# Edge counts of a graph attention from 16 buckets instead of 8 tiles, with one matmul per block of edges

## The reference, cut to what matters

```python
# x: (1024, 512); src, dst: (17408,) node numbers
edge_index = jnp.stack([src, dst])
xn = _layernorm(x, axis=-1)
q = xn @ Wq + bq;  k = xn @ Wk + bk;  v = xn @ Wv + bv
adj = zeros((N, N)).at[edge_index[0], edge_index[1]].set(1.0)
a = q @ k.T / sqrt(512)
a = a * adj + (1.0 - adj) * NEG
x = x + softmax(a, axis=-1) @ v
...
# a later stage, the same edges: neigh = segment_sum(feat[src], dst)
```

## Time and profile before

| | |
|---|---|
| runs | 1079.86, 1082.82, 1085.95 us; median 1082.82 |
| profiled execution | 1079.54 us, span 1077.7 us |
| granted TensorE clock, mean | 0.919 of full speed |
| TensorE busy | 887.4 us (82%) |
| VectorE busy | 758.5 us (70%) |
| ScalarE busy | 506.9 us (47%) |
| GpSimd busy | 357.5 us (33%) |
| first stage up to the first transpose of its attention | 246.8 us |

### The profile page before, as it was taken

One profiled execution on the slowest core, in us unless ns is written; L12 is line 12 of the kernel. 1 busy time (PEld: TensorE's weight loads), 2 busy tenths in 40 slices (PEclk: granted clock), 3 DMA queues, 4 the chain that ended last, 5 costly groups with the idle time before them and its releaser, 6 DMA issues.

```text
span 1077.7 us, 13803 instructions
## 1 busy us (share of the span) xinstructions
PE 887.4 (82%) x4522; PEld 676.1 (63%) x4522; DVE 758.5 (70%) x1555; ACT 506.9 (47%) x881; POOL 357.5 (33%) x236
## 2 busy tenths in 40 slices
PE   2999998888883999698898689899999987655990
PEld 2777773336762887377686567777767765434860
DVE  8879599886697443866223767788786867796638
ACT  3467517655653555122202146656565655543530
POOL 1000000000112553008320337786685666703520
PEclk9999999998986999599998899999999998967985
DMA  5110000007252443623210330020010140373442
GB/s 161 30 22 2 1 1 1 1 16 259 79 201 82 136 149 117 245 66 110 62 46 1 107 78 1 20 59 20 2 30 20 21 156 1 101 261 96 149 145 89
DMA packets 55524, 84.74 MB, mean 79 GB/s; under 512 B 8977, under 2 KB 31761, under 8 KB 54945
## 3 DMA queue, kind: packets, MB, share of 16 engines
q1 hardware_dynamic: 49376, 63.94, 19.0%
q0 software_dynamic: 6080, 19.93, 5.7%
HBM read 57.11 MB, written 22.54 MB: 74 GB/s over the span
## 4 chain that ended last, share of the span: by engine, by line
PE 56%; DVE 33%; ACT 4%; issue 4%; POOL 1%; DMA 1%; DVEq 0%; ACTq 0%; POOLq 0%
PE PS L328 36%; DVE late_columns L1153 4%; PE PS L1980 3%; PE PS L1995 3%; DVE neg_max L1553 3%; PE PS L1969 3%; DVE APL L987 2%; PE PS L1994 2%; DVE count_rows L1133 2%; PE PS L1888 2%; PE PS L1669 2%; PE PS L1831 2%; DVE early_columns L1153 1%; DVE XN L1024 1%; DVE stats L995 1%
## 5 line engine op out<-in xcount | busy, mean ns | idle before, releaser
L616 POOL TENSOR_SCALAR AP__201<-AP__201,rden 128x1024 f32<-128x1024 f32 x64 | 182.0, 2848 | 86.4 <-DVE rden L1558 85.8
L557 POOL TENSOR_TENSOR W1L<-W1R,W1H 128x1024 fp32r<-128x1024 f32 x8 | 18.9, 2404 | 291.5 <-DVE neg_max L1172 288.5
L648 ACT ACTIVATE APH<-PS 128x512 fp32r<-128x512 f32 x128 | 71.7, 597 | 70.2 <-PE PS L1980 45.7
L1553 DVE TENSOR_REDUCE neg_max<-PS 128x1 f32<-128x1024 f32 x64 | 78.3, 1223 | 36.9 <-PE PS L1969 36.0
L987 DVE TENSOR_TENSOR APL<-PS,APH 128x512 fp32r<-128x512 f32 x128 | 83.0, 680 | 23.8 <-ACT APH L648 23.6
L328 PE MATMUL PS<-XTH,WH 128*128 128x512 f32 x224 | 79.9, 403 | 4.5 <-DVE XTL L987 4.5
L1980 PE MATMUL PS<-ident,AP__201 128*128 128x128 f32 x512 | 71.2, 281 | 11.5 <-DVE APL L987 10.7
L1980 PEld LDWEIGHTS PS<-ident,AP__201 128*128 128x128 f32 x512 | 59.9, 144 | 28.2 <-issue 17.1
L328 PE MATMUL PS<-XTL,WH 128*128 128x512 f32 x224 | 77.2, 391 | 0.0
L328 PE MATMUL PS<-XTH,WL 128*128 128x512 f32 x224 | 77.0, 390 | 0.0
L928 ACT ACTIVATE AP__201<-PS,neg_max 128x1024 f32<-128x1024 f32 x64 | 71.5, 1117 | 7.3 <-DVE neg_max L1553 6.6
(11 more groups left out here) (302 smaller groups left out, 2422.1 us busy)
## 6 DMA issues: line engine op xcount, KB each, us to landing
YT<-expert_rows SPq DMA_DIRECT2D x12, 512.0 KB, 7.5
counts<-CT SPq DMA_DIRECT2D x8, 512.0 KB, 4.9
W1R<-in_L_ffn_w SPq DMA_DIRECT2D x8, 512.0 KB, 3.9
W2R<-in_L_ffn_w SPq DMA_DIRECT2D x8, 512.0 KB, 5.3
normalised<-XN SPq DMA_DIRECT2D x2, 2048.0 KB, 8.4
CG<-counts SPq DMA_DIRECT2D x8, 512.0 KB, 3.4
RAW<-in_L_gnn_W SPq DMA_DIRECT2D x16, 256.0 KB, 2.9
W1R<-in_L_ffn_W SPq DMA_DIRECT2D x8, 512.0 KB, 8.7
```

Of the source, the lines that this page charges most:

```text
L616: gp.tensor_scalar(AP_[:, i % 4, :], AP_[:, i % 4, :], rden[:, i % 4:i % 4 + 1], None, ALU.mult).then_inc(B["norm"], 1)
L648: act.activation(dst, src, Copy, **kw).then_inc(s, 1)
L1553: v.tensor_reduce(out=neg_max[:, i % 4:i % 4 + 1], in_=banks(2 * (i % 2)), axis=X_AXIS, op=ALU.max, negate=True).then_inc(B["mx"], 1)
```

## The change

The sorted list now has 16 buckets: the row tile (8) and the half of the columns (2). Bucket 2t is tile t with columns 0 to 511. An edge's column is kept within its half (`dst & 511`). A block belongs to one bucket, so it needs only one product of 512 columns. Sixteen padded buckets make 152 blocks. `RING`, the number of groups of four column matrices in flight, goes from 8 to 6, and VectorE makes all columns; ScalarE's two-step columns are gone.

The 16 buckets share eight banks: bucket k uses bank k % 8. ScalarE copies a finished bucket out (`count_out`), and for the first eight it then clears the bank by a copy with scale 0. Which bucket a block belongs to is known only at run time, so two sequences of waits on register values are added: SP loads each bucket's last group and signals `bucket_done`; POOL loads how many banks each pair of groups needs, waits until as many are free, and signals `banks_granted`, for which TensorE waits.

The sorting steps are placed anew among VectorE's projection steps, `lanes()` begins after block 3 and not after block 0, and TensorE's `move_edges` begins in block 5 and not in block 2; the remaining quads go behind every k step of the first score tiles. The bias of V is added per tile within the attention. ScalarE loads its table for the exponential ahead of the last bucket.

```diff
-    EDGE_BLOCKS = EC + NT
+    BUCKETS = 2 * NT
+    EDGE_BLOCKS = EC + BUCKETS
...
-    RING = 8
-    SORTS = (5, 23)
+    RING = 6
+    SORTS = (7, 18, 29)
+    PLACED = SORTS[2] + 6
...
# SP
-        wait(columns_used, 2 * COUNT_GROUPS)
+        wait(sort_dve, PLACED)
+        for k in range(BUCKETS - 1):
+            last = sp.value_load(last_group[0:1, k:k + 1], min_val=1, max_val=COUNT_GROUPS)
+            wait(columns_used, last)
+            sp.sem_inc(bucket_done, 1)
+        wait(columns_used, COUNT_GROUPS)
...
# POOL
+        wait(sort_dve, PLACED)
+        for g in range(COUNT_GROUPS // 2):
+            needed = gp.value_load(banks_needed[0:1, g:g + 1], min_val=1, max_val=BUCKETS)
+            wait(bank_free, needed)
+            gp.sem_inc(banks_granted, 1)
...
# ACT
-            if i:
+            if i >= 4:
                 steps()
-            steps()
+            if i >= 3:
+                steps()
...
+        def count_out(k):
+
+            if k < BUCKETS - 1:
+                act.wait_ge(bucket_done, k + 1)
+            else:
+                act.wait_ge(columns_used, COUNT_GROUPS)
+            copy(CT[:, k // 2, k % 2 * HALF:(k % 2 + 1) * HALF], PS[:, k % 8, :], counted)
+            if k < 8:
+                act.wait_ge(counted, k + 1)
+                copy(PS[:, k, :], PS[:, k, :], bank_free, scale=0.0)
...
+        for k in range(BUCKETS):
+            count_out(k)
+            if k in (1, 3):
+                no_edge(0, k // 2)
+            if k == BUCKETS - 2:
+                act.activation(inv[:, 0:1], neg_col[:, 0:1], ACT.Exp, scale=-1.0)
...
# DVE
         projected(0)
...
+        bucket_bases()
+        projected(1)
+        places()
+        projected(2)
+        edge_columns()
+        projected(3)
         lanes()
-        for i in range(1, 2 * KT):
+        for i in range(4, 2 * KT):
             projected(i)
+            if i == 5:
+                banks_of_blocks()
             lanes()
             lanes()
...
-        for r in range(2):
-            for g in range(COUNT_GROUPS):
...
-                for j in range(4 - g % 2):
...
+        for k in range(COUNT_GROUPS):
+            if k >= RING:
+                v.wait_ge(columns_used, k - RING + 1)
+            elif k == 2:
+                v.wait_ge(Q0["s_ps"], NT)
+            for j in range(4):
+                b = 4 * k + j
+                got = v.tensor_scalar(count_columns(k, j), columns16[:, 0:HALF], block_rc[:, 1, b:b + 1], None, ALU.is_equal)
+            got.then_inc(columns_ready, 1)
...
# PE
-                if i >= 2 and k % 2:
+                if i >= 5 and k % 2:
                     move_edges()
...
-                if k % 2 and moved[0] < QUADS:
+                if moved[0] < QUADS:
                     move_edges()
...
+            if g % 2 == 0:
+                pe.wait_ge(banks_granted, g // 2 + 1)
+            pe.wait_ge(columns_ready, g + 1)
+            for j in range(4):
+                b = 4 * g + j
+                got = pe.matmul(PS[:, ds(held[b % 24]), :].rearrange("p a n -> p (a n)"), count_rows[:, b, :],
+                                count_columns(g, j), start=False, stop=False, skip_group_check=True)
+            got.then_inc(columns_used, 1)
```

More of the change, by code:

```diff
@@ L272, in build @@
     rows_ready, columns_ready, columns_used = sem("rows_ready"), sem("columns_ready"), sem("columns_used")
[L273 to L274 removed]
+    bank_free, banks_granted, bucket_done = sem("bank_free"), sem("banks_granted"), sem("bucket_done")
+    counted = sem("counted")
     raw_in = [sem(f"raw_in{s}") for s in range(4)]
@@ L430, in _ @@
         results(0)
-        wait(Q0["bias"], 1)
+        wait(Q0["bias"], NT)
         sp.dma_start(row0[:, :], a["L1_gnn_b2"].partition_broadcast(P)).then_inc(row0_in, 16)
@@ L700, in _ @@
         for t in range(NT):
+            for _ in range(min(3, QUADS - stepped[0])):
+                steps()
             act.wait_ge(Q0["s_ps"], t + 1)
             copy(SR[:, t, :], banks((4, 0)[t % 2]), Q0["s_done"], scale=-D ** -0.5)
-            for _ in range(min(2, QUADS - stepped[0])):
-                steps()
         assert stepped[0] == QUADS
[L707 to L729, removed]
-        for i in range(2 * per_round):
-            if i + 1 < 2 * per_round:
-                column_distance(i + 1)
-            column(i)
-            if i == per_round + 1:
-                counts_out(0)
-        counts_out(1)
+        def count_out(k):
[7 more added lines that the diff above has]
+                copy(PS[:, k, :], PS[:, k, :], bank_free, scale=0.0)
         def no_edge(half, par):
             t = 2 * half + par
-            act.wait_ge((counted_act, counted_dve)[par], NT // 2 + half + 1)
+            act.wait_ge(counted, 2 * t + 2)
             if t >= 2:
@@ L1129, in _ @@
         sort(v.tensor_tensor(block_rc[:, :, :], block_sum[:, :, 1:STEPS_OF], block_sum[:, :, 0:EDGE_BLOCKS], ALU.subtract))
-        sort(v.tensor_scalar(minus_column[:, :], block_rc[:, 1, :], -1.0, None, ALU.mult))
         v.wait_ge(Q0["v_ps"], NT)
@@ L1187, in residual @@
             v.wait_ge(A["rden"], t + 1)
+            v.wait_ge(Q0["bias"], t + 1)
             x = X[:, ds(t), :].rearrange("p a n -> p (a n)")
@@ L1654, in _ @@
         pe.wait_ge(setup, 12)
-        pe.wait_ge(sort_dve, SORTS[0])
-        pe.matmul(PS[:, 6, 0:NT], before16[:, :], tile_count16[:, :], start=True, stop=True)
-        pe.matmul(PS[:, 6, NT:2 * NT], ones16[:, :], tile_count16[:, :], start=True, stop=True).then_inc(sort_ps, 1)
         moved = [0]
```

188 lines of the change are left out of this document (92 added, 96 removed).

## The result

The changed kernel took 1039.49 us in the median of its runs (1037.90 to 1045.57); the kernel before took 1082.87 beside it (1079.86 to 1085.95). The ratio is 0.961, with a 95% interval of 0.9569 to 0.9651. The forecast was 1041.2.

A forecast was written before the change was run, and what follows sets the result against it. It took TensorE to bound the kernel until the edges were done, then VectorE, with both full in the columns. Its terms summed to -41.65 us from 1079.54, giving 1037.9, or 1041.2 on the median's scale; 8-in-10 range 1034 to 1053.

The forecast's parts named there:

- Start: Before the layer norm: with the scan moved behind the transposes, VectorE starts the statistics near 7.55, gaining 0.65 us if x is there.
- The new wait at block 4: Projections: TensorE waits 1.25 us for VectorE's low half of block 2, delayed by moved sorting steps; bounds 0 and 4.
- Moving the edges: Projections to first score tiles: 34 wider edge groups cost TensorE 1.0 us more; no stall, upper bound 5 us; edges end 134.85.
- Between the edges and the columns: From block_sum to columns: -0.2 for block steps, +1.3 for eight more count_rows, -7.4 for table work and bias gone.
- The columns: Counting: 152 VectorE columns at 0.263 take 40.0 us, plus 3.9 to first transpose, against 81.3 before: -37.4 us.
- The grants: Counting: the added waits and register loads of POOL and SP stay hidden, cost 0; paid from 2.1 us up.
- Attention: Eight value bias steps of 0.55 to 0.6 us hide in VectorE's wait ahead of PTL, except the last: +0.45 us.
- a cheaper restart: Rival, 12%: TensorE's clock holds through the gap before attention, first transposes save 0.9 and first values 1.7 us: 1038.6.
- Clock: Rival, 5%: pauses in each counting group hold TensorE at 1.2 GHz, so transposes come 30 us later: 1071.
- alternation: Rival, 2%: POOL's load gets through only when VectorE pauses, so both engines take turns in the columns: 1109, slower than before.
- grants cost: Rival, 6%: a POOL round trip of 2.5 to 3 us in the counting costs 19 x 0.4 to 0.9: 1049 to 1058.
- The cover fails: Rival, 15%: places, lanes or biases in VectorE's queue each run a little long and are no longer hidden: 1046 to 1050.

The follow-up runs named there:

- first profile: The changed kernel, profiled beside its first timing against the kernel before: profiled execution 1045.57 us, the slowest of its runs; median 1039.49 us.
- second profile: The changed kernel run again without an edit, for a second trace: profiled execution 1039.11 us; median 1043.34 us, ratio 0.9633 to the kernel before.
- both: Changed kernel with VectorE making three of four column matrices and TensorE's counting products 256 instead of 512 columns wide (counts wrong): 1037.47 us, ratio 0.959.
- both_load8: Changed kernel with three of four columns made, 256-column products, and TensorE loading 32 bank numbers per eight groups, not 24 per six: 1037.77 us, ratio 0.9582.

## Why the prediction was right, step by step

**Start.** -0.65 forecast. In the first profile it came: 7.43 against 8.21, -0.78 by VectorE, -0.6 by TensorE's first matmul (27.17 against 27.79). In the second it did not: the first half of x landed 6.4 us after its issue and not 5.6, VectorE waited 0.60 us for it, the statistics began at 8.11 and the first matmul at 27.76. That is the condition of the prediction (it counts only if x is there), and it differs between executions of one program.

**The new wait at block 4.** 1.25 forecast, 1.14 measured in both profiles (in the first TensorE was done with block 3 at 51.19, had one small matmul for the sorting, and began block 4 at 52.50). In the first profile TensorE came 2.1 us late from its first matmuls (7.55 us for 5.5), and VectorE, which has to wait for the same block, was late by as much; in the second these took 5.75, and the wait was the same. So it was no luck. There is a slip in my working: four blocks of 24 matmuls at 13.90/60 take 22.2 us, so block 3 would end at 49.4 and not at 49.1, and the wait would be 0.95.

**Moving the edges.** +1.0 forecast, and 0.56 us a group in the steady stretch as the sum has it. The edges ended 3.4 us later than forecast in the first profile and 2.2 in the second. The step that failed is that TensorE's work before the edges' end was taken at the pace of before throughout. In the first profile 2 us went in the first 24 matmuls; in the second these took 5.75 but began at 27.76, 0.6 later than forecast. In both, some 1.6 went at the start of V, where the clock of 80 to 88 was 0.79 (1.00 before) and eight edge matmuls took 1.05. Neither has to do with the lanes: TensorE did not wait for them. That no slip came at the moves was right, but the argument was too short. I compared rates (1.67 us of lanes against 1.97 a group) and called the bound of 5 us generous. The cover is the third group that VectorE has ordered ahead of TensorE, not the rate; without it the price is 15 us, three times that bound.

**Between the edges and the columns.** Forecast -0.2 + 1.3 - 7.4 = -6.3 us. From block_sum to the first column it took 25.86 us; before, 165.48 - 133.28 = 32.20. That is -6.34. The third group of columns did not wait for the last score.

**The columns.** Forecast 40.0 and 3.9 to the first transpose, measured 40.1 and 3.8 (208.06 - 204.24). The 1.05 us at 169.47 is in the chain, but VectorE itself stood for only some 0.1 us of it. The claim that both engines are full held too: TensorE's last products ended about 1.8 us behind VectorE's last column, just early enough not to delay the exponential; an earlier start of TensorE gave nothing, a quarter fewer columns 0.9. The half-width products gave 0.2 us, but they did not relieve TensorE. For TensorE's side my term was 0.4 us a load; the pauses are 0.34 to 0.5 and once 1.04, so it was right in size. But it was right only because 0.216 us products hide the rest of a load of 2.3 us.

**The grants.** Nothing forecast. The kernel with constant waits measured nothing for the loads, and TensorE waited for no grant.

**Attention.** +0.45 forecast; from the first to the last residual 49.26 us against 48.70, +0.56. The bias steps vanished into the wait for PTH as said.

**The sum.** -41.65 forecast. Against the second profile: 1039.11 - 1079.54 = -40.4. The difference of 1.2 is +2.2 for the edges, -0.2 for the columns' stretch, -1.4 for the attention, and +0.5 behind it. The -1.4 is the rival "a cheaper restart": from the first transpose to the first residual it took 10.28 us in the second profile and 11.60 in the first (11.78 before). Both outcomes occur for the same program, so it was no case of its own but a part of the scatter.

**The rivals.** *Clock*, *alternation* and *grants cost* fell. The rule of the Trainium skill named in the prediction (TensorE: Matmul & The Clock Gate, "A second HAM failure mode: psum-queue depth-cycling") did not decide here: products went round eight PSUM banks with pauses of up to 1 us, and the granted clock of 165 to 200 was 1.00. With pauses of 2.3 us, in `both`, it was 0.90, and one run of 16 products took 3.51 us instead of 2.27; what pushed it down cannot be told from these runs. The other rule of the Trainium skill (SBUF — State Buffer, "Who interferes with whom") cost nothing either: POOL loaded its registers beside VectorE's columns, and constants in their place changed nothing. *The cover fails* did not come to pass, though one group less in hand would have brought it, at three times its price.

**Left open.** What made the start of V slow. Ten profiles come from kernels that share the change's code up to there. In eight of them the first edge matmuls of V took 1.05 us, but in `both` and `both_load8` 0.55, and in those two the first 24 matmuls of the projections had taken 7.8. The two profiles with the projections of before had 0.53. TensorE's wait just ahead of V is no explanation: it stood idle for 2.57 us there in after and for 2.59 before. No experiment was made to remove it.

## What to carry to other kernels

Where two engines fill a stage alike, only an edit that takes work from both moves it, and the sum is then one multiplication: count the remaining operations of the slower one by their duration. Count with each engine all that stands in its queue: a test that makes its operations shorter relieves it only if the trace shows its cycle shorter too. For work that is passed between engines under a loop, compare the loop and not the rates: write down the chain from one hand-over to the next and see how many items must be in hand to break it. An operation that is cheap behind long neighbours, such as a register load behind wide matmuls, has to be priced anew when the neighbours shrink.

## What was not expected of the hardware

- A register load by TensorE costs 0.09 to 0.1 us for each number where nothing hides it (1.1 to 1.2 us for 12, 2.3 for 24, 3.0 for 32), and mostly 0.3 to 0.6 us for 24 behind matmuls of 512 columns.
- The first 24 matmuls of the projections took 5.75 us in some executions and 7.1 to 7.8 in others of nearly the same code.
- Two executions of one kernel differed by 3.9 us in a part that no edit touched, so a single profile of it can mislead by as much as the smaller terms of the sum.
